# Self attention of layer 0: a head as four equal steps of scores, maxima, values and pieces

## The chip, the cores and the metric

The kernel runs on one core of a Trainium2 chip. The metric is device time in microseconds (us), the median of some runs. TensorE (PE) does the matmuls, VectorE (DVE), ScalarE (ACT) and GpSimd (POOL) the elementwise work, and SyncE (SP) issues nearly all transfers of this stage. Each engine works off its own instructions in their order; only weight loads (PEld) run beside matmuls.

## The reference, cut to what matters

Two decoder layers, each with self attention, cross attention and a feed-forward part, each followed by a sum with its input and a layer norm. The change touches the first self attention alone. Its input is x, 4 sequences of 1024 tokens with 256 features, and the reshape makes it 64 independent attentions of 1024 by 1024 with 64 features:

```python
SCALE = HEAD_DIM ** (-0.5)
bsz, seqlen, _ = x.shape
xq = jnp.einsum('bsh,oh->bso', x, wq)
xk = jnp.einsum('bsh,oh->bso', x, wk)
xv = jnp.einsum('bsh,oh->bso', x, wv)
xq = xq.reshape(bsz, N_HEADS, seqlen, HEAD_DIM)
...
scores = jnp.einsum('bhid,bhjd->bhij', xq, xk) * SCALE
scores = jax.nn.softmax(scores, axis=-1)
out = jnp.einsum('bhij,bhjd->bhid', scores, xv)
out = out.reshape(bsz, seqlen, N_HEADS * HEAD_DIM)
return jnp.einsum('bso,ho->bsh', out, wo)
...
x = _layernorm(x + _L0_attn_ref(x, L0_attn_wq, L0_attn_wk, L0_attn_wv, L0_attn_wo), axis=-1)
```

## The kernel before

`layer0_self_attention` (L301) takes 64 heads, in 16 groups of four (j = 0 to 3; GT = 256 tokens of x make one group). q and k are kept as a high and a low part in fp32r, and the products of scores are made of these. For a head the tiles are kA (high over low part of k), qA (high part of q twice), kB and qB (high part of k and low part of q; the first eight rows of kB are ones, those of qB the masked row maxima). Each is double buffered by the parity of the head.

A head does, per tile kc of 128 keys (kc = 0 to 7):
- scores (L614): two matmuls with kA, qA ("A") and two with kB, qB ("B"), all L627, into the four banks of psS, two for even and two for odd kc;
- the exponent (L639, ACT) from psS into pr, a ring of four tiles of 128x1024, and the sum of the exponents on POOL (add_up, L655; none for kc 0);
- values (L658): the product of pr and vd into psO (L667), 64 columns of the array for each half of the queries. These matmuls are fp32 and show as eight records for two kc.

Between them runs the work for the next head. largest (L567) takes 16 products (L579) of that head into the two banks of psX, of which VectorE takes the row maximum at once (L584); each waits for the maximum before the last. At the end of the head max_rows (L588) turns these maxima with two transposes into psX (L594), VectorE joins them (L599, L600), and masked (L605, L609) writes them into qB, half by half. The B matmuls of kc 0 wait for that.

The third kind of work are the pieces (misc, L395), products for a later group: 16 of Q and K in a group (L417: six matmuls, the high part taken out by ACT in L458, the low part by VectorE in L462, then sent to DRAM), V four times (L425, ACT L471), T, the transposes of x (L407), and O, the output product of two heads (L436, out by VectorE in L482, then moments, root and norm_out). S (L430) adds up the sums of exponents with ones; L475 turns it. They go to bank psM or, where it is free, to psX. Where they stand is the table SLOTS, by head and a name for the place; the waits for their bank are counted (`back`, `under`).

The order of a head before: scores 0 to 3 with largest 0 to 7, piece "1", values 0 and 1, S of the head before; scores 4 and 5 with largest 8 to 11, values 2 and 3, pieces "2" and "2b"; scores 6 and 7 with largest 12 to 15 (V pieces between); values 4 to 7; take_out (L677, psO to oU); max_rows; then the rest of the pieces, with the halves of masked among them:

```python
if more and not rest_first:
    masked(w, nb, 0)
    masked(w, nb, 1)
past_3 = piece("3")
if more and rest_first and (j, "3e") not in SLOTS:
    masked(w, nb, 0)
past_3b = piece("3b", bank=psX[:, 1, :], under=past_3)
if more and rest_first and (j, "3e") in SLOTS:
    masked(w, nb, 0)
```

rest_first holds where piece "3" is one of Q or K. Head 0 ends in two pieces and O, head 1 in four and V, head 2 in T and O, head 3 in five pieces. build (L531) fetches the tiles of the head after next when the last scores of a head are through: six transfers of 256 KB on SP, four of which (semaphore a0 or a1) the first L579 of the next head waits for. build_v (L556) fetches vd. divide (L696, POOL) applies the reciprocal of the sums.

## Time and profile before

| | before |
|---|---|
| median of 3 runs | 2968.56 us (2965.77 to 2969.53) |
| the profiled execution, its span | 2978.0 us |
| PE busy | 2631.8 us, 88% |
| DVE busy | 1704.5 us, 57% |
| POOL busy | 1621.4 us, 54% |
| ACT busy | 1190.8 us, 40% |
| adds of exponents, L655, 384 and 64 | 914.8 and 153.3 us |
| row maxima, L584, 1024 | 694.2 us |
| products of values, L667, 2048 records | 481.8 us |
| products of maxima, L579, 1024 | 415.8 us |

The busy times are of the whole program, of which the stage in question is the first 1760 us or so. The span is that of one profiled execution, the slices of the page cut it into 40 equal parts. A start time in a timeline is in us from the start of the span; where several equal instructions follow each other they are one row with a count.

### The profile page before, as it was taken

To read this page: it belongs to the slowest core of one execution; us is meant where nothing else is said; L and a number is where in the kernel's file an instruction comes from. 1 tells how busy PE (TensorE), PEld (TensorE's weight loads), DVE (VectorE), ACT (ScalarE), POOL (GpSimd) and SP (SyncE) were. 2 spreads that over 40 slices of the span, in tenths; PEclk is the share of its full clock that TensorE was granted. 3 is DMA by queue.
4 is the path that set the end of the run, shared out by engine and by line. 5 is a ranking of instruction groups with operands and counts; after the bars stand their busy time and mean duration, and the time that the engine had idled before them with its cause. 6 is when DMAs were issued, how large, how long until landed. Compare 5 with 4: busy or idle time off the path is not lost. (4 is left out here: it accounts for less than half of the span.)

```text
span 2978.0 us, 43667 instructions
## 1 busy us (share of the span) xinstructions
PE 2631.8 (88%) x12081; PEld 1634.0 (55%) x12081; DVE 1704.5 (57%) x3436; ACT 1190.8 (40%) x1678; POOL 1621.4 (54%) x1343
## 2 busy tenths in 40 slices
PE   7999999999999999999999968982795588798695
PEld 5666666666666666666666534441574244454254
DVE  5666666656666666665666635662234555468743
ACT  3444444444444444444444324541222333454234
POOL 3666776767766677676776753424334313333343
PEclk8999999999999999999999979996897599899798
DMA  6565455555446445455544320003993100000232
GB/s 176 113 136 113 105 120 113 123 115 114 109 113 138 108 109 121 109 122 114 118 112 108 76 68 23 2 2 126 343 347 128 41 0 1 30 2 9 61 116 88
DMA packets 407010, 303.20 MB, mean 102 GB/s; under 512 B 293558, under 2 KB 338910, under 8 KB 401790
## 3 DMA queue, kind: packets, MB, share of 16 engines
q1 hardware_dynamic: 390734, 231.17, 33.1%
q0 software_dynamic: 12224, 64.71, 6.1%
q10 hardware_dynamic: 3952, 6.08, 0.6%
q8 instruction: 51, 0.84, 0.1%
q14 instruction: 49, 0.40, 0.0%
HBM read 187.04 MB, written 94.39 MB: 95 GB/s over the span
## 5 line engine op out<-in xcount | busy, mean ns | idle before, releaser
L655 POOL TENSOR_TENSOR a_total<-a_total,a_pr 128x1024 f32<-128x1024 f32 x384 | 914.8, 2382 | 46.1 <-ACT a_pr L639 23.4
L639 ACT ACTIVATE a_pr<-a_psS 128x1024 f32<-128x1024 f32 x512 | 525.3, 1027 | 657.3 <-PE a_psS L627 657.3
L584 DVE TENSOR_REDUCE a_nmax<-a_psX 128x1 f32<-128x512 f32 x1024 | 694.2, 687 | 139.9 <-PE a_psX L579 137.8
L667 PE MATMUL a_psO<-a_pr,a_vd 128*64 128x512 f32 x2048 | 481.8, 602 | 0.0
L579 PE MATMUL a_psX<-a_kA,a_qA 128*128 128x512 f32 x1024 | 415.8, 408 | 17.3 <-issue 6.2
L655 POOL TENSOR_TENSOR a_total<-a_pr 128x1024 f32<-128x1024 f32 x64 | 153.3, 2396 | 487.9 <-ACT a_pr L639 487.9
L627 PE MATMUL a_psS<-a_qA,a_kA 128*128 128x512 f32 x1024 | 339.1, 412 | 2.5 <-DVE a_nT L600 1.4
L627 PE MATMUL a_psS<-a_qB,a_kB 128*128 128x512 f32 x1024 | 322.1, 396 | 0.0
L667 PEld LDWEIGHTS a_psO<-a_pr,a_vd 128*64 128x64 f32 x2048 | 129.9, 136 | 239.6 <-issue 188.1
L579 PEld LDWEIGHTS a_psX<-a_kA,a_qA 128*128 128x128 f32 x1024 | 193.9, 189 | 102.2 <-DVE a_nmax L584 23.5
L627 PEld LDWEIGHTS a_psS<-a_qA,a_kA 128*128 128x128 f32 x1024 | 181.2, 189 | 121.5 <-issue 90.1
L627 PEld LDWEIGHTS a_psS<-a_qB,a_kB 128*128 128x128 f32 x1024 | 193.6, 189 | 41.3 <-DVE a_qB L609 2.8
L599 DVE COPY a_nT<-a_psX 8x128 f32<-8x128 f32 x64 | 17.8, 278 | 222.4 <-PE a_psX L594 222.4
L1119 DVE TENSOR_REDUCE c_nmx<-c_psM 128x4 f32<-128x308 f32 x256 | 109.7, 469 | 50.9 <-PE c_psM L1114 50.0
L475 DVE STREAM_TRANSPOSE a_turned<-a_psM 128x512 f32<-128x512 f32 x64 | 45.9, 717 | 139.0 <-PE a_psM L430 139.0
L677 ACT ACTIVATE a_oU<-a_psO 128x512 f32<-128x512 f32 x64 | 38.4, 599 | 184.1 <-PE a_psO L667 180.1
L1103 POOL CAST c_qR<-c_qF 128x512 fp32r<-128x512 f32 x64 | 40.3, 632 | 113.7 <-ACT c_qF L1098 113.6
L609 DVE TENSOR_TENSOR a_qB<-a_nT,a_rowmask 8x512 fp32r<-8x512 f32 x128 | 99.3, 787 | 0.7
L1114 PE MATMUL c_psM<-c_kblk,c_qR 128*128 128x308 f32 x256 | 78.0, 369 | 23.5 <-DVE c_nmx L1119 10.1
L2607 ACT ACTIVATE e_hT<-e_psH,e_wt 128x128 f32<-128x128 f32 x160 | 45.7, 368 | 131.9 <-PE e_psH L2599 125.9
L1269 POOL TENSOR_TENSOR c_rstd<-c_mv,c_eps 128x2 f32<-128x2 f32 x32 | 6.6, 206 | 166.3 <-DVE c_mv L1259 166.3
L1114 PEld LDWEIGHTS c_psM<-c_kblk,c_qR 128*128 128x128 f32 x256 | 45.0, 193 | 90.2 <-issue 83.2
(400 smaller groups left out, 4517.5 us busy)
## 6 DMA issues: line engine op xcount, KB each, us to landing
a_qA<-a_qhi SPq DMA_DIRECT2D x124, 256.0 KB
a_vd<-a_vg SPq DMA_DIRECT2D x128, 128.0 KB
a_kA<-a_khi SPq DMA_DIRECT2D x62, 256.0 KB
a_kA<-a_klo SPq DMA_DIRECT2D x62, 256.0 KB
a_kB<-a_khi SPq DMA_DIRECT2D x62, 256.0 KB, 5.6
a_qB<-a_qlo SPq DMA_DIRECT2D x62, 256.0 KB, 5.9
a_qhi<-a_ph SPq DMA_DIRECT2D x120, 128.0 KB, 3.2
a_qlo<-a_pl SPq DMA_DIRECT2D x120, 128.0 KB, 2.7
```

The lines of the kernel that those rows point to most:

```text
L475: w.eng.transpose(turned[:, :], ps[:, :]).then_inc(sems["md"], 1)
L579: w.eng.matmul(psX[:, half, :], qA[:, b, u * P:(u + 1) * P], kA[:, b, half * 512:(half + 1) * 512], start=True, stop=True).then_inc(sems[" ...
L584: w.eng.tensor_reduce(nmax[:, half, u:u + 1], psX[:, half, :], AX.X, ALU.max, negate=True)\
L609: w.eng.tensor_tensor(qB[0:KC, b, cols].rearrange("p (u q) -> p u q", q=P), nT[:, 1, :].unsqueeze(1).to_broadcast([KC, KC // 2, P]), rowma ...
L627: last = w.eng.matmul(psS[:, half, q, :], kt[:, b, kc * P:(kc + 1) * P], qt[:, b, q * 512:(q + 1) * 512], start=a == 0, stop=a == 1)
L639: w.eng.activation(pr[:, n, :], psS[:, half, :, :].rearrange("p a b -> p (a b)"), ACT.Exp, scale=SCALE)\
L655: w.eng.tensor_tensor(total[:, buf, :], first, pr[:, n, :], ALU.add).then_inc(sems["ad"], 1)
L667: last = w.eng.matmul(psO[q * HD:(q + 1) * HD, :], vd[:, b, kc, :], pr[:, n, q * 512:(q + 1) * 512], start=kc == 0, stop=kc == KC - 1)
L1103: w.eng.tensor_copy(qR[:, n % 2, c, :], qF[:, n % 3, c, :]).then_inc(sems["qr"], 1)
L1114: w.eng.matmul(psM[:, k, 0:K4], qR[:, n % 2, c, tt * P:(tt + 1) * P], kblk[:, c, b, :, :].rearrange("p i k -> p (i k)"), start=True, stop= ...
L1119: w.eng.tensor_reduce(nmx[:, tt, 4 * c:4 * c + 4], psM[:, k, 0:K4].rearrange("p (i k) -> p i k", k=TK), AX.X, ALU.max, negate=True).then_i ...
L2607: last = w.eng.activation(hT[:, par, a, :], psH[:, par, a, :], GELU, bias=wt[:, slot, B1 + a:B1 + a + 1])
```

## The change

The table SLOTS and its places give way to TASKS, by head and step. A head is four equal steps p: scores 2p and 2p+1, with four of the 16 products of largest; then two kc of values, those of the step before (in step 0 kc 6 and 7 of the head before, and then take_out); S in step 1; then the pieces of the step. scores and exponent are apart. The pieces of Q and K: in head 3 two, none, two, four; in head 0 two, none, none, four; in head 1 two in step 0. V stands in step 2 of heads 0 and 1 and twice in that of head 2, O at the end of heads 1 and 2 (behind T there). With the last step go max_rows and masked: half 0 directly, half 1 directly or behind the third piece. moments stand in step 0, root in step 1, turn_back, divide and norm_out in step 2.

The waits for a bank are kept in `w.came`, the semaphore and count that took out what was last in it; room waits for that. build becomes two: build_keys behind step 1 (three transfers of half a tile, 128 KB) and build behind step 3 (nine of them; semaphore a needs its first four and the three of build_keys, b the other five). Before the loop eight pieces of Q and K are made for group 1, and sent by POOL, instead of five, and the waits of TensorE for all pieces ahead of the first head go. Shapes and number of the matmuls stay as they are.

```diff
-        AHEAD = 5
+        AHEAD = 8
         QK = [("Q", c) for c in range(KC)] + [("K", c) for c in range(KC)]
-        PLACES = [(3, "3"), (3, "3b"), (3, "3c"), (3, "3d"), (3, "3e"), (0, "1"), (0, "2"), (0, "2b"), (0, "3"), (0, "3b"),
-                  (1, "1"), (1, "3"), (1, "3b"), (1, "3c"), (1, "3e"), (2, "1")]
-        SLOTS = task_list()
+        PLACES = [(3, 0), (3, 0), (3, 2), (3, 2), (3, 3), (3, 3), (3, 3), (3, 3), (0, 0), (0, 0), (0, 3), (0, 3), (0, 3), (0, 3),
+                  (1, 0), (1, 0)]
+        TASKS = {place: [] for place in PLACES}
+        for place, task in zip(PLACES, QK, strict=True):
+            TASKS[place].append(task)
+        TASKS[0, 2], TASKS[1, 2], TASKS[2, 2] = [("V", 0, 0)], [("V", 0, 1)], [("V", 1, 0), ("V", 1, 1)]
+        TASKS[1, 3], TASKS[2, 3] = [("O", 1)], [("T",), ("O", 0)]
+        BANKS = {("QK", 2): "1M", ("QK", 4): "M10M", ("V", 1): "M", ("V", 2): "1M", ("O", 1): "M", ("T", 2): "1M"}
+        bank = {"0": psX[:, 0, :], "1": psX[:, 1, :], "M": psM[:, :]}
+        bank.update((f"S{i}", psS[:, i // 2, i % 2, :]) for i in range(4))
...
-        def misc(w, what, G, buf, more=True, bank=None, back=(0, 0), out=True):
+        def room(w, *places):
+
+            least = {}
+            for name, value in (w.came[k] for k in places if k in w.came):
+                least[name] = max(least.get(name, 0), value)
+            for name, value in least.items():
+                w.wait(name, w.at(name, w.count[name] - value))
+
+        def misc(w, what, G, buf, k="M", more=True, out=True):
 
 
             kind = what[0]
-            ps = psM if bank is None else bank
-            if w.on("tensor"):
-                w.wait("md", w.at("md", back[0]))
-                w.wait("ma", w.at("ma", back[1]))
+            ps = bank[k]
+            if w.on("tensor"):
+                room(w, k)
...
+            w.came[k] = ("ma", w.count["ma"]) if kind in "TV" else ("md", w.count["md"])
...
-        def build(w, G, j, b):
+        def halves(t, rows, b, h):
+            return t[rows:rows + HD, b, h * 512:(h + 1) * 512].bitcast(F32)
+
+        def build_keys(w, G, j, b):
+
 
             if w.on("sync"):
                 row = w.fixed(G * (GH * P) + j * P)
-                w.waits(("s", w.at("s")), ("sg", AHEAD * 2 * 16), ("sh", (PIECES - AHEAD) * 2 * 16), *((f"so{n}", w.at(f"so{n}")) for n in range(PIECES)))
-                for t, rows, src, n in ((qA, 0, qhi, "a"), (kA, 0, khi, "a"), (qA, HD, qhi, "a"), (kA, HD, klo, "a"),
-                                        (kB, HD, khi, "b"), (qB, HD, qlo, "b")):
-                    w.eng.dma_start(t[rows:rows + HD, b, :].bitcast(F32).rearrange("p (s n) -> p s n", n=512),
-                                    src[bass.ds(row, P), :].rearrange("(s p) n -> p s n", p=HD)).then_inc(sems[f"{n}{b}"], 16)
+                if j == 0:
+                    w.waits(("sg", AHEAD * 2 * 16), ("sh", (PIECES - AHEAD) * 2 * 16), *((f"so{n}", w.at(f"so{n}")) for n in range(PIECES)))
+                w.waits(("s", w.at("s")))
+                for t, rows, src in ((kB, HD, khi), (kA, 0, khi), (kA, HD, klo)):
+                    w.eng.dma_start(halves(t, rows, b, 0), src[bass.ds(row, HD), :]).then_inc(sems[f"a{b}"], 16)
+            w.inc(f"a{b}", 3 * 16)
+
+        def build(w, G, j, b):
+
+
+            if w.on("sync"):
+                row = w.fixed(G * (GH * P) + j * P)
+                w.waits(("s", w.at("s")))
+                for h, t, rows, src, n in ((0, qA, 0, qhi, "a"), (0, qA, HD, qhi, "a"), (1, kA, 0, khi, "a"), (1, kA, HD, klo, "a"),
+                                           (1, qA, 0, qhi, "b"), (1, qA, HD, qhi, "b"), (1, kB, HD, khi, "b"), (0, qB, HD, qlo, "b"),
+                                           (1, qB, HD, qlo, "b")):
+                    w.eng.dma_start(halves(t, rows, b, h), src[bass.ds(row + h * HD, HD), :]).then_inc(sems[f"{n}{b}"], 16)
             w.inc(f"a{b}", 4 * 16)
-            w.inc(f"b{b}", 2 * 16)
+            w.inc(f"b{b}", 5 * 16)
...
-        def largest(w, i, b, back=None):
+        def largest(w, i, b, first=False):
 
 
             u, half = i // 2, i % 2
             if w.on("tensor"):
                 if i == 0:
-                    w.wait(f"fa{b}", 8 * 16)
+                    if first:
+                        w.wait(f"fa{b}", 8 * 16)
+                        w.wait(f"fb{b}", 4 * 16)
                     w.wait(f"a{b}", w.at(f"a{b}"))
-                    w.wait("mn", w.at("mn"))
-                if back is not None:
-                    w.wait("md", w.at("md", back))
-                w.wait("mxr", w.at("mxr", 1))
+                elif i == KC:
+                    w.wait(f"b{b}", w.at(f"b{b}"))
+                room(w, "01"[half])
                 w.eng.matmul(psX[:, half, :], qA[:, b, u * P:(u + 1) * P], kA[:, b, half * 512:(half + 1) * 512],
                              start=True, stop=True).then_inc(sems["mx"], 1)
             w.inc("mx")
@@ -584,12 +612,13 @@
                 w.eng.tensor_reduce(nmax[:, half, u:u + 1], psX[:, half, :], AX.X, ALU.max, negate=True)\
                     .then_inc(sems["mxr"], 1)
             w.inc("mxr")
-
...
-        def scores(w, kc, b, a):
-
-            half = kc % 2
-            if w.on("tensor"):
-                if a == 0:
-                    if kc == 0:
-                        w.wait(f"fb{b}", 4 * 16)
-                        w.wait(f"b{b}", w.at(f"b{b}"))
-                    w.wait("e", w.at("e", 1))
-                kt, qt = (kB, qB) if a else (kA, qA)
-                for q in range(2):
-                    if a and kc == 0:
-                        w.wait("mb", w.at("mb", 1 - q))
-                    last = w.eng.matmul(psS[:, half, q, :], kt[:, b, kc * P:(kc + 1) * P], qt[:, b, q * 512:(q + 1) * 512],
-                                        start=a == 0, stop=a == 1)
-                if a:
-                    last.then_inc(sems["s"], 1)
-            if a == 0:
-                return
-            w.inc("s")
+        def scores(w, p, b, nb, first=False):
+
+
+            for kc in (2 * p, 2 * p + 1):
+                if w.on("tensor"):
+                    room(w, f"S{2 * (kc % 2)}", f"S{2 * (kc % 2) + 1}")
+                    w.wait("e", w.at("e", 1 - kc % 2))
+                for a, (kt, qt) in enumerate(((kA, qA), (kB, qB))):
+                    if w.on("tensor"):
+                        for q in range(2):
+                            if a and kc == 0:
+                                w.wait("mb", w.at("mb", 1 - q))
+                            last = w.eng.matmul(psS[:, kc % 2, q, :], kt[:, b, kc * P:(kc + 1) * P], qt[:, b, q * 512:(q + 1) * 512],
+                                                start=a == 0, stop=a == 1)
+                        if a:
+                            last.then_inc(sems["s"], 1)
+                    if nb is not None:
+                        largest(w, 2 * kc + a, nb, first)
+            for i in range(4):
+                w.came.pop(f"S{i}", None)
+            w.inc("s", 2)
+
+        def exponent(w, kc):
+
             n = w.count.get("e", 0) % RING
             if w.on("scalar"):
-                w.wait("s", w.at("s"))
-                w.wait("pv", w.at("pv", {0: 3, 1: 2}.get(kc, 1 - kc % 2)))
+                w.wait("s", w.at("s", 1 - kc % 2))
+                w.wait("pv", w.at("pv", 1 - kc % 2))
                 w.wait("ad", w.at("ad", 3 if kc in (0, 5, 6, 7) else 2))
-                w.eng.activation(pr[:, n, :], psS[:, half, :, :].rearrange("p a b -> p (a b)"), ACT.Exp, scale=SCALE)\
+                w.eng.activation(pr[:, n, :], psS[:, kc % 2, :, :].rearrange("p a b -> p (a b)"), ACT.Exp, scale=SCALE)\
                     .then_inc(sems["e"], 1)
             w.inc("e")
 
...
+            def tasks(j, p):
...
+                normal = j == 3 or (j == 2 and not first)
+                nG, nbuf = (G, 0) if j == 3 else (G - 1, 1)
+                for p in range(KC // 2):
+                    scores(w, p, b, nb if more else None, first and j == 0)
+                    for kc in (2 * p, 2 * p + 1):
+                        exponent(w, kc)
+                        add_up(w, kc, j % 2)
+                    if p == 0 and normal:
+                        moments(w, nbuf)
+                    if p == 0 and j == 2 and left >= 2:
+                        load_x(w, G + 2)
+                    if p == 1 and normal:
+                        root(w, nbuf)
+                    if p == 2 and old:
+                        turn_back(w)
+                        divide(w, (j - 1) % GH)
+                    if p == 2 and normal:
+                        norm_out(w, nG, nbuf)
+                    if not (last and j >= 2):
+                        if p == 1:
+                            build_keys(w, G + (j + 2) // GH, (j + 2) % GH, b)
+                        if p == 3:
+                            build(w, G + (j + 2) // GH, (j + 2) % GH, b)
+                    if p == 0:
+                        if old:
+                            values(w, KC - 2, nb)
+                            values(w, KC - 1, nb)
+                            take_out(w)
+                        if more:
+                            build_v(w, (j + 1) % GH, nb)
                     else:
...
                         values(w, 2 * p - 2, b)
                         values(w, 2 * p - 1, b)
-                        if p == 1 and old:
-                            misc(w, ("S",), G, (j + 1) % 2)
-                        if p == 1 and more:
-                            build_v(w, (j + 1) % GH, nb)
-                    if p == 2:
-                        under = piece("2")
-                        if w.on("tensor") and (j, "2b") in SLOTS:
-                            w.wait("mxr", w.at("mxr"))
-                        piece("2b", bank=psX[:, 1, :], under=under)
-                for kc in range(KC - 4, KC):
-                    values(w, kc, b)
-                take_out(w)
-                if more:
-                    max_rows(w, nb)
-                rest_first = left > 0 and SLOTS.get((j, "3"), ("T",))[0] in "QK"
-                if more and not rest_first:
-                    masked(w, nb, 0)
-                    masked(w, nb, 1)
-                past_3 = piece("3")
-                if more and rest_first and (j, "3e") not in SLOTS:
-                    masked(w, nb, 0)
-                past_3b = piece("3b", bank=psX[:, 1, :], under=past_3)
...
+                    if p == 1 and old:
+                        misc(w, ("S",), G, (j + 1) % 2)
+                    todo = tasks(j, p)
+                    if p == 3 and more:
+                        max_rows(w)
+                        masked(w, nb, 0)
+                        if not todo or todo[0][0][0] not in "QK":
+                            masked(w, nb, 1)
+                    for n, (task, g, buf) in enumerate(todo):
+                        kind = "QK" if task[0] in "QK" else todo[0][0][0]
+                        misc(w, task, g, buf, BANKS[kind, len(todo)][n] if len(todo) < 3 or kind == "QK" else "M")
+                        if p == 3 and more and n == 2:
+                            masked(w, nb, 1)
...
-            if w.role == "tensor":
-                w.wait("md", w.at("md"))
             for i in range(2 * KC):
-                largest(w, i, 0)
+                largest(w, i, 0, True)
...
             for i in range(AHEAD):
-                misc(w, QK[i], 1, 1, bank=psS[:, i // 2, i % 2, :] if i < 4 else psM[:, :], back=(i, 0))
+                misc(w, QK[i], 1, 0, ("S0", "S1", "S2", "S3", "M")[i % 5])
                 if i == 1:
-                    max_rows(w, 0)
+                    max_rows(w)
                     masked(w, 0, 0)
                     masked(w, 0, 1)
-            if w.role == "tensor":
-                w.wait("md", w.at("md"))
             group(w, 0, first=True)
...
+            values(w, KC - 2, 1)
+            values(w, KC - 1, 1)
+            take_out(w)
```

## Rows read from the trace of the kernel before

**Rows 1.** The page: the span, and the granted TensorE clock in 40 slices.

```profile
span 2978.0 us, 43667 instructions
PEclk8999999999999999999999979996897599899798
```

**Rows 2.** Four heads by stretches, 846.40 to 952.55: the sum; busy us of each engine.

```profile
sum 106.15, PE 105.51 PEld 67.32 DVE 65.43 ACT 45.53 POOL 73.63; mean PE 26.38 PEld 16.83 DVE 16.36 ACT 11.38 POOL 18.41
```

**Rows 3.** Timeline of PE: start, us, engine, line, operation, out<-in, shape, count; scores after O.

```profile
829.49 0.40 PE L579 MATMUL a_psX<-a_kA,a_qA 128*128 128x512 f32 x1
829.72 0.62 PE L627 MATMUL a_psS<-a_qA,a_kA 128*128 128x512 f32 x2
830.44 0.50 PE L579 MATMUL a_psX<-a_kA,a_qA 128*128 128x512 f32 x1
830.77 0.63 PE L627 MATMUL a_psS<-a_qB,a_kB 128*128 128x512 f32 x2
831.24 0.40 PE L579 MATMUL a_psX<-a_kA,a_qA 128*128 128x512 f32 x1
```

**Rows 4.** Timeline of PE, start of a head behind five pieces.

```profile
902.65 0.49 PE L579 MATMUL a_psX<-a_kA,a_qA 128*128 128x512 f32 x1
...
904.21 0.62 PE L627 MATMUL a_psS<-a_qA,a_kA 128*128 128x512 f32 x2
```

**Rows 5.** Timeline of PE, pieces and the product O behind them.

```profile
821.16 0.40 PE L417 MATMUL a_psX<-a_xl,a_wkh 128*128 128x256 f32 x2
821.40 0.40 PE L417 MATMUL a_psX<-a_xh,a_wkl 128*128 128x256 f32 x2
822.02 3.72 PE L436 MATMUL a_psM<-a_wo,a_oT 128*128 128x256 f32 x16 [0.22 <-DVE a_pl L462]
```

**Rows 6.** Timeline of PE, a short block of values and the long one.

```profile
837.64 0.39 PE L579 MATMUL a_psX<-a_kA,a_qA 128*128 128x512 f32 x1
...
839.83 0.74 PE L627 MATMUL a_psS<-a_qA,a_kA 128*128 128x512 f32 x2
840.41 0.40 PE L579 MATMUL a_psX<-a_kA,a_qA 128*128 128x512 f32 x1
...
842.49 0.39 PE L579 MATMUL a_psX<-a_kA,a_qA 128*128 128x512 f32 x1
...
846.40 0.38 PE L594 MATMUL a_psX<-a_ident,a_nmax 128*8 128x128 f32 x2
```

**Rows 7.** Line L609, 100 to 1600: duration in ns, min/median/max, first and last start.

```profile
L609 DVE TENSOR_TENSOR a_qB<-a_nT,a_rowmask x114: 669/670/1450, 105.3 to 1593.2; 8x512 fp32r<-8x512 f32 x114
```

**Rows 8.** Timeline of POOL and of DVE, end of a head 3.

```profile
896.76 4.84 POOL L655 TENSOR_TENSOR a_total<-a_total,a_pr 128x1024 f32<-128x1024 f32 x2
...
900.98 1.17 DVE L609 TENSOR_TENSOR a_qB<-a_nT,a_rowmask 8x512 fp32r<-8x512 f32 x1
```

**Rows 9.** Timeline, all engines: the B pair of a kc and its exponent.

```profile
1701.39 0.63 PE L627 MATMUL a_psS<-a_qB,a_kB 128*128 128x512 f32 x2
...
1702.05 1.02 ACT L639 ACTIVATE a_pr<-a_psS 128x1024 f32<-128x1024 f32 x1 [0.37 <-PE a_psS L627]
```

**Rows 10.** Timeline, PE and DVE: the transposes of the maxima and the masks.

```profile
1691.63 0.38 PE L594 MATMUL a_psX<-a_ident,a_nmax 128*8 128x128 f32 x2
...
1692.67 3.43 DVE L609 TENSOR_TENSOR a_qB<-a_nT,a_rowmask 8x512 fp32r<-8x512 f32 x2
```

**Rows 11.** Timeline of PE, last group: last B pair and the next head's first L579.

```profile
1687.26 0.62 PE L627 MATMUL a_psS<-a_qB,a_kB 128*128 128x512 f32 x2
...
1695.26 0.67 PE L579 MATMUL a_psX<-a_kA,a_qA 128*128 128x512 f32 x1 [1.84 <-issue]
```

**Rows 12.** Transfers issued from 800 to 1000: count, KB each, median us to landing.

```profile
a_kB<-a_khi SPq DMA_DIRECT2D x7, 256.0 KB, 5.6
...
y_scratch<-a_res SPq DMA_DIRECT2D x4, 128.0 KB, 1.7
```

**Rows 13.** Timeline of PE, start of the second head.

```profile
82.63 0.47 PE L579 MATMUL a_psX<-a_kA,a_qA 128*128 128x512 f32 x1 [1.45 <-issue]
```

102 lines of the change are left out of this document (29 added, 73 removed).

## The prediction

> **What bounds the kernel now.** I read the page first. Its slices show that the first stage, the self attention of layer 0, fills the first 24 of 40, at a granted TensorE clock of 0.9 or more of full speed, and that nothing behind it uses a line of the diff; the chain of the page speaks of the last stage only, so it is no help here [rows 1]. The table by stretches, cut at the transposes of L594 (one per head), is the view to trust: the four heads of a group take 106.15 us, TensorE is busy for 105.51 of them, VectorE for 65, ScalarE for 46 and GpSimd for 74 [rows 2]. So a head costs what TensorE's program costs, and another engine counts only where TensorE waits for it. Busy time hides short waits, because the ends of matmuls are modelled; I read the distance from one start to the next instead. In a run of scores that is 0.23 for one L579 (829.49 to 829.72) and 0.47 for a pair of L627 (830.77 to 831.24) [rows 3].
>
> **What the change removes.** The number and shape of all products stay: no line changes values(), S, the transposes or the pieces (values still fill 64 columns at a time), so any gain must come from waits. I find three kinds.
> (a) Where a head is entered after the product O, eight L579 in a row run into VectorE, which has the result of O and its moments between the maxima: the pair at 829.72 takes 0.72 for 0.47 and the L579 behind it 0.33 for 0.23, so 0.36 in all. Two heads of a group, 16 groups: 11.5 us. After the change only four L579 stand in a row, and the moments stand behind them, beside a block of values. I count this as gone.
> (b) Behind the five pieces at the end of head 3 the next head goes from 902.65 to 904.21, 1.56 for 0.23+0.47+0.23, so 0.63 lost [rows 4]; 14 groups, 8.8 us.
> (c) O waits for a piece in its own bank: 0.62 for 0.24, so 0.38 [rows 5]; 15 groups, 5.7 us. It gets a head end without pieces, and what was in its bank before was taken out long ago.
> Together 26 us.
>
> **What it adds: a fourth block of half array products.** Before, a head has values 0-1 (with S), 2-3 and 4-7; after, 6-7, 0-1 with S, 2-3 and 4-5. Crossing between the whole array and the halves is paid in each. A short block (8 products) goes from 837.64 to 839.83, less 0.23 for the L579 itself: 1.96; the pair of scores behind it then takes 0.58, 0.12 too much. The long one (16) goes from 842.49 to 846.40, less 0.23: 3.68, and the transposes behind it pay nothing [rows 6]. Two short ones are 1.96+0.12+1.96=4.04, so the split costs 0.36, in 63 heads 22.7 us. No reason is in the trace for less: each of the three blocks of a head pays it now.
> The Trainium skill has two rules that speak here against each other. "TensorE: Matmul & The Clock Gate" (Step-by-step) says that the engine loads weights ahead of running matmuls; by that alone the fourth block is free and the sum 22.7 us lower. "TensorEngine Tiling (Array Packing)" (Key Properties) says that a change of tiling mode drains the engine. The distances above side with the second.
>
> **What it moves: the mask before the pieces.** This is the largest term. At the end of a head the row maxima are turned, then L609 writes them into qB in two halves. Before, the halves stand behind the first pieces on VectorE; after, masked(0) stands ahead of all of them. L609 reads two operands from SBUF, as does GpSimd's add L655. The median of 114 masks is 0.67, the longest 1.45 [rows 7]. Where one meets an add, it ends 0.55 behind that add: POOL's pair of adds ends at 901.60, the mask that began at 900.98 at 902.15 [rows 8]. Now the clock of the new end of head 3 or head 0, from the start of scores 6:
> scores 6 are A 0.46, L579 0.23, B pair from 0.69; the exponent starts 0.66 behind the start of that pair and takes 1.02 [rows 9]: it ends at 2.4. Adds take 2.4 each [rows 8]: the add of 6 runs from 2.5 to 4.9, that of 7 from 4.9 to 7.3. TensorE ends scores 7 at 2.8, does its short block until 4.7 and turns the maxima. The mask starts 1.04 behind the transposes (1691.63 to 1692.67) [rows 10], at 5.8, in the middle of the last add: it ends at 7.85. Before, four kc of values stood there, and the mask meets the adds in one head of each group, that of rows 8.
> Who waits for that: VectorE is in order, so piece 0 is taken out (0.42) only by 8.3. TensorE needs that for the fourth piece, which has bank M again; it ends three pieces, nine pairs 0.24 apart [rows 5], at 4.7+0.2+3x0.72=7.1. So it stands for 1.2. The reductions of the next head start late and cost 0.1 more. In head 3 the root of the norm (four small POOL operations, 1.3 us) and the division push the adds by another 0.3 to 0.4. I take 1.5. It happens behind head 3 (14 times) and head 0 (15): 43 us. Its bounds: nothing, if the add is out of the way; 2.4 (a whole further add) if POOL is later than I think, 70 us. I take the middle because both ends of the overlap have room: the mask would have to start 0.9 earlier or 1.5 later to miss that add. Behind heads 1 and 2 stands O (3.3 us), under which both masks fit; no cost.
> The Trainium skill ("SBUF — State Buffer", Who interferes with whom) has it that a VectorE instruction with two SBUF inputs and a GpSimd instruction that reads SBUF exclude each other for a whole instruction. The trace agrees.
>
> **What else moves.** The tiles of the head after next are now fetched by 12 transfers of half the size in place of 6, three of them after step 1 and nine after step 3. SyncE has room, since none of its steps is asked for sooner than a step later, except the four that the first L579 of the next head needs. From the pair of scores 7 to that L579 now pass up to 8.0 us (1687.26 to 1695.26), where a head end without other work shows the transfers alone in the way [rows 11]. After the change, behind O of head 1, the window from the end of scores 7 is 6.1, as two kc of values less stand in it; behind head 2 6.6, behind pieces 6.8 and more. Transfers of 256 KB land 5.6 after issue with others before them in the queue, one of 128 KB after 1.7 [rows 12]. Half the bytes, and four issues in place of four twice as long: I take 5 and call it hidden; the other end is no gain in speed, 1.1 at most behind head 1, 0.6 behind head 2 and less elsewhere, 14x1.1+16x0.6+32x0.2 to 0.4, some 30 us in all.
> Setting up: eight pieces in place of five before the first head is the same work earlier. One wait of 1.45 at the second head may go, since half the bytes are in its transfers [rows 13]; with the wait for all pieces ahead of the first head, I count 2 us less. The last two groups have head ends without pieces, where masks and adds meet anyway: TensorE leaves one block of values less there and pays it later, 1 us in two places, 2 us more. POOL bounds the very last head in both.
>
> **Sum.** -26 (waits) +22.7 (fourth block) +43 (mask) -2 +2 = +39.7 us. The profiled execution has 2978.0; the median of the runs is 2968.56, 9.4 lower, and I add the difference to the median: 3008.3. A group in the middle should take 106.15-(2x0.36+0.63+0.38)+4x0.36+2x1.5=108.9.
>
> **Rivals.**
> 1. The mask doesn't meet the add, or the piece doesn't wait for the mask: 43 us fall away and the sum is -5: 2964, not slower. It decides itself at the start of masked(0): before 4.9 or after 7.3 in the clock above. For it: three of four head ends now are clean. Against it: these have 1.7 us more of values ahead. 0.17.
> 2. The fetch of the next head's tiles is late (it takes the place of the waits that went): up to +30, 3038. For it: the present slack is 1 us or less in a plain head end. Against it: half the bytes. 0.12.
> 3. The blocks cost nothing more, by the weights loaded ahead: 3008.3-22.7=2985.6. Against it: rows 6. 0.04.
> 4. The pace of single matmuls changes, as it varies from 0.226 to 0.236 within a head for no cause that I can name: 0.004 on some 216 of them in a group is 14 us: 2994, or 2951 together with rival 1. 0.05, 0.03 of it on the fast side.
> The forecast: 0.60, with its own range from 2994 to 3023 (a stall of 1.0 to 2.0 in 29 places). 0.02 is left for what makes it faster and stands nowhere above.
>
> **How the numbers follow.** A difference under 0.2%, 5.9 us, can't be told from none here. Faster: rival 1 has -5 with some 4 either way, so 0.08 of its 0.17, with 0.03 of rival 4 and the 0.02: 0.13. Same: the other 0.09 of rival 1. Slower: the rest, 0.78. The range must reach to rival 1 and most of the way to rival 2: 2962 to 3030.
>
> **What would show it.** Between transposes: heads 3 and 0 longer, heads 1 and 2 about as now, group 108.9. In the lines: L609 at 1.5 to 2.1 in half of its first halves, a wait of L417 for L462 of some 1.2, 29 times; no wait of L579 for a reduction inside a step. A wait of L579 for the tiles of kA would be rival 2. I am wrong if the masks stay at 0.67, or if the group is under 106.

## The result, and the profile after

| | before | after |
|---|---|---|
| median | 2968.77 us (2965.77 to 2969.53, 4 runs) | 3036.55 us (3033.16 to 3042.03, 4 runs) |
| profiled span | 2978.0 us | 3035.6 us |
| VectorE busy | 1704.5 us | 1802.9 us |
| masks of the row maxima, 128 (L609, now L639) | 99.3 us, 787 ns each | 185.9 us, 1472 ns each |

The ratio is 1.0229, 95% interval 1.0213 to 1.0246: slower by 67.8 us, where 39.7 had been forecast, and above the upper end of the range, 3030. The sign was right and the size was not.

The four heads that answer to [rows 2], from the transposes at the end of one head 1 to those at the end of the next (the table by stretches; the columns are the busy time and the count of each engine, the granted clock, the share of the DMA engines, GB/s):

```profile
core 0: us, PE busy (x) PEld busy (x) DVE busy (x) ACT busy (x) POOL busy (x), PEclk, DMA share, GB/s
882.36:910.50 28.14, 26.58 (x116) 16.30 (x114) 16.88 (x27) 10.48 (x12) 18.86 (x13) 1.00 0.29 89
910.50:937.62 27.12, 27.12 (x132) 17.31 (x131) 18.94 (x32) 11.91 (x16) 18.71 (x13) 1.00 0.42 110
937.62:965.26 27.64, 26.34 (x131) 16.40 (x129) 18.21 (x29) 11.69 (x16) 18.08 (x9) 1.00 0.50 125
965.26:992.66 27.40, 26.28 (x130) 16.45 (x128) 17.98 (x29) 11.70 (x16) 17.87 (x9) 1.00 0.50 124
sum 110.30, PE 106.32 PEld 66.46 DVE 72.00 ACT 45.78 POOL 73.52; mean PE 26.58 PEld 16.61 DVE 18.00 ACT 11.45 POOL 18.38
```

The group takes 110.30 us for 106.15, and 108.9 had been forecast. TensorE is busy for 0.8 more and stands still for 3.98 in place of 0.64. VectorE's busy time has grown by 6.57. Three of the four stretches have a hole in TensorE's row of 1.1 to 1.6 us, and only the second has none.

The waits of TensorE (waiting operation and its line, what released it, us in total, times, longest) name the holes:

```profile
PE a_psM L426 <- DVE a_pl L472: 35.1, 29, 1.4
PE a_psO L701 <- DMA a_vd<-a_vg: 20.9, 15, 1.6
...
PE a_psX L607 <- issue: 5.9, 1, 5.9
```

The first is the piece (L426) that waits until VectorE has emptied its bank, 29 times as forecast. The second stood nowhere in the forecast: the first product of values of a head waits for a transfer into vd. The third is the first product of the program's first head.

The first hole, at the end of a head 3 (timelines of DVE, POOL and PE; start, us, engine, line):

```profile
828.31 2.44 DVE L639 TENSOR_TENSOR a_qB<-a_nT,a_rowmask 8x512 fp32r<-8x512 f32 x1
830.68 0.41 DVE L472 TENSOR_TENSOR a_pl<-a_psM,a_ph 128x256 fp32r<-128x256 f32 x1
...
825.37 4.84 POOL L689 TENSOR_TENSOR a_total<-a_total,a_pr 128x1024 f32<-128x1024 f32 x2
...
829.39 0.40 PE L426 MATMUL a_psX<-a_xh,a_wql 128*128 128x256 f32 x2
831.14 0.50 PE L426 MATMUL a_psM<-a_xh,a_wqh 128*128 128x256 f32 x2 [1.35 <-DVE a_pl L472]
```

It answers to [rows 8] and reads as the forecast has it: the mask begins at 828.31, GpSimd's pair of adds ends at 830.21, the mask at 830.75, 0.54 behind it; only then is piece 0 taken out, and the fourth piece, due at 829.63, starts at 831.14. That is 1.51 lost; behind head 0 it is 1.28; the pair behind each hole takes 0.35 for 0.24 (831.14 to 831.49), another 0.1. Over 100 to 1600 the median of the masks is 1378 ns where [rows 7] has 670. Behind heads 1 and 2 the first half of the mask is as long (median 2.17 and 2.18), but no piece of Q or K waits behind it there.

The second hole, in step 1 of a head 2 (timelines of SyncE's queue and of PE):

```profile
890.64 0.40 SPq L391 DMA_DIRECT2D a_xg<-x  x1
891.14 0.42 SPq L393 DMA_DIRECT2D a_xs<-x  x1
891.74 1.14 SPq L589 DMA_DIRECT2D a_vd<-a_vg  x2
...
893.43 0.40 PE L607 MATMUL a_psX<-a_kA,a_qA 128*128 128x512 f32 x1
895.38 1.94 PE L701 MATMUL a_psO<-a_pr,a_vd 128*64 128x512 f32 x8 [1.56 <-DMA a_vd<-a_vg]
```

The transfers that are awaited here are not those that values 0 read. build_v in step 0 fetches the values of the next head, into the buffer that values 7 of the old head leave. The values that values 0 multiply were fetched a head earlier, and landed by 867.3. The two pairs of transfers (instructions of one line: count, min/median/max in ns, first and last start):

```profile
L589 SPq DMA_DIRECT2D a_vd<-a_vg x2: 506/548/591, 864.4 to 864.9; - x2
...
DMA to landing us min/median/max: 2.2/2.3/2.4
```

```profile
L589 SPq DMA_DIRECT2D a_vd<-a_vg x2: 495/542/590, 891.7 to 892.3; - x2
...
DMA to landing us min/median/max: 3.1/3.1/3.1
```

The second pair lands at 895.34, and values 0 start at 895.38. The reason is in the wait of values(), which the change left as it was:

```python
if kc == 0:
    w.wait("bv", w.at("bv"))
```

w.at counts all transfers that the program has issued so far. In the kernel before, build_v stands behind values 0 and 1 in step 1, so the count takes in only the head's own; now it stands in step 0, and the count takes in the next head's too. Those are late in head 2 for two reasons: they can't be issued before values 7 are through (888.90+1.94=890.84), and the fetch of x stands ahead of them on SyncE until 891.56. No piece stands in this step 0 to cover the wait. So values 0 start 1.95 behind the L607 ahead of them, where 0.32 is usual: 1.63 in each group.

The third, the first product of maxima of all, after and before (timeline of PE):

```profile
40.42 1.19 PE L607 MATMUL a_psX<-a_kA,a_qA 128*128 128x512 f32 x2 [5.92 <-issue]
```

```profile
36.18 0.92 PE L579 MATMUL a_psX<-a_kA,a_qA 128*128 128x512 f32 x2 [2.26 <-DMA a_kA<-a_pl]
```

The change makes it wait for all twelve transfers of the first head and not for the eight that it reads, and the first transposes come 4.5 us later, at 56.75 for 52.27.

### The profile page after: what moved, and what is told of

It reads as the page before. It is cut to its first block and busy times, and to the rows that moved or that the text cites. A ratio compares the mean times of both kernels' runs of the same rounds, so it can differ in the third digit from the quotient of the medians.

```text
span 3035.6 us, 43749 instructions
## 1 busy us (share of the span) xinstructions
PE 2638.9 (87%) x12081; PEld 1616.4 (53%) x12081; DVE 1802.9 (59%) x3436; ACT 1194.3 (39%) x1678; POOL 1622.4 (53%) x1349
## 5 line engine op out<-in xcount | busy, mean ns | idle before, releaser
L701 PE MATMUL a_psO<-a_pr,a_vd 128*64 128x512 f32 x2048 | 496.7, 606 | 21.0 <-DMA a_vd<-a_vg 20.9
L607 PE MATMUL a_psX<-a_kA,a_qA 128*128 128x512 f32 x1024 | 410.3, 402 | 13.6 <-issue 5.9
L656 PE MATMUL a_psS<-a_qA,a_kA 128*128 128x512 f32 x1024 | 336.1, 409 | 0.2 <-DVE a_pl L472 0.2
L656 PE MATMUL a_psS<-a_qB,a_kB 128*128 128x512 f32 x1024 | 322.9, 396 | 4.1 <-DVE a_qB L639 4.0
L607 PEld LDWEIGHTS a_psX<-a_kA,a_qA 128*128 128x128 f32 x1024 | 194.6, 190 | 80.2 <-DVE a_nmax L612 11.4
L656 PEld LDWEIGHTS a_psS<-a_qA,a_kA 128*128 128x128 f32 x1024 | 180.5, 189 | 99.3 <-issue 70.6
L656 PEld LDWEIGHTS a_psS<-a_qB,a_kB 128*128 128x128 f32 x1024 | 193.5, 189 | 43.8 <-DVE a_qB L639 6.4
L639 DVE TENSOR_TENSOR a_qB<-a_nT,a_rowmask 8x512 fp32r<-8x512 f32 x128 | 185.9, 1472 | 2.2
L472 DVE TENSOR_TENSOR a_pl<-a_psX,a_ph 128x256 fp32r<-128x256 f32 x120 | 47.3, 413 | 124.8 <-ACT a_ph L468 124.8
L446 PE MATMUL a_psM<-a_wo,a_oT 128*128 128x256 f32 x512 | 117.6, 383 | 3.3 <-POOL a_oT L730 3.3
L446 PEld LDWEIGHTS a_psM<-a_wo,a_oT 128*128 128x128 f32 x512 | 96.0, 193 | 17.4 <-issue 5.0
L468 ACT ACTIVATE a_ph<-a_psM 128x256 fp32r<-128x256 f32 x119 | 45.7, 384 | 130.9 <-PE a_psM L426 130.9
```

Source lines behind the costliest of these rows:

```text
L446: last = w.eng.matmul(ps[:, 0:D], oT[:, buf, c, :], wo[:, c, :], start=c == 0, stop=c == KC - 1)
L607: w.eng.matmul(psX[:, half, :], qA[:, b, u * P:(u + 1) * P], kA[:, b, half * 512:(half + 1) * 512], start=True, stop=True).then_inc(sems[" ...
L639: w.eng.tensor_tensor(qB[0:KC, b, cols].rearrange("p (u q) -> p u q", q=P), nT[:, 1, :].unsqueeze(1).to_broadcast([KC, KC // 2, P]), rowma ...
L656: last = w.eng.matmul(psS[:, kc % 2, q, :], kt[:, b, kc * P:(kc + 1) * P], qt[:, b, q * 512:(q + 1) * 512], start=a == 0, stop=a == 1)
L701: last = w.eng.matmul(psO[q * HD:(q + 1) * HD, :], vd[:, b, kc, :], pr[:, n, q * 512:(q + 1) * 512], start=kc == 0, stop=kc == KC - 1)
```

## The experiments

All medians are set against runs of the kernel before on the same chip. What stands over it is the ratio less one, times 2969 us.

| run | median us | ratio, 95% interval | over the kernel before |
|---|---|---|---|
| the changed kernel | 3036.55 | 1.0229 (1.0213 to 1.0246) | +68 |
| e2_mask_psum | 3009.88 | 1.0134 (1.0114 to 1.0155) | +40 |
| e3_mask_late | 3004.73 | 1.0117 (1.0096 to 1.0137) | +35 |
| e7_before_mask_first | 3010.84 | 1.0129 (1.0113 to 1.0144) | +38 |
| e4_vd_four | 3012.97 | 1.0144 (1.0118 to 1.0170) | +43 |
| e5_first | 3035.95 | 1.0206 (1.0185 to 1.0226) | +61 |
| e10_three_mended | 2989.50 | 1.0046 (1.0031 to 1.0061) | +14 |
| e6_four_blocks | 3042.71 | 1.0222 (1.0201 to 1.0243) | +66 |
| e1_values_home | 3001.44 | 1.0109 (1.0089 to 1.0130) | +32 |
| e9_home_apart | 3120.05 | 1.0495 (1.0476 to 1.0513) | +147 |
| e11_apart_early | 2978.86 | 1.0017 (1.0007 to 1.0027) | +5 |
| e12_pair_early | 2954.83 | 0.9961 (0.9948 to 0.9974) | -12 |

**The mask: where it reads, and what is queued behind it.** The same wait was attacked from two sides. First the operand:

```diff
-w.eng.tensor_tensor(nT[:, 1, :], nT[:, 0, :], psX[0:KC, 0, P:2 * P], ALU.min)
+w.eng.tensor_tensor(psX[0:KC, 0, 2 * P:3 * P], nT[:, 0, :], psX[0:KC, 0, P:2 * P], ALU.min)
...
-                    nT[:, 1, :].unsqueeze(1).to_broadcast([KC, KC // 2, P]),
+                    psX[0:KC, 0, 2 * P:3 * P].unsqueeze(1).to_broadcast([KC, KC // 2, P]),
...
                         masked(w, nb, 0)
-                        if not todo or todo[0][0][0] not in "QK":
-                            masked(w, nb, 1)
+                        masked(w, nb, 1)
...
+            w.came["0"] = ("mb", w.count["mb"])
```

> The changed kernel, except that the minimum of the two halves of the row maxima is written to PSUM, so that the mask (L639) reads one operand from PSUM and one from SBUF, as the reductions do; both masks of a head stand behind one another, and the bank they read is free only after both. Everything else, the blocks and the add on GpSimd, is as in the changed kernel. Theory (the mask waits for the whole GpSimd add because both read two operands in SBUF): the masks go back to about 0.7 in all heads, the fourth piece's stall of 1.3 to 1.5 us mostly goes; a part of it comes back since the second mask (0.7) now stands ahead of the pieces: -14 to -28 us, 3008 to 3022. Rival (the mask is long for another reason: the wait on its inputs, its own write to qB, or the place in the order): first halves stay above 2 us, and with the second ahead of the pieces the time is 3036 or more, up to 3056.

The masks of e2 (costliest groups: busy us, mean ns) and the wait that is left:

```profile
L639 DVE TENSOR_TENSOR a_qB<-a_psX,a_rowmask 8x512 fp32r<-8x512 f32 x128 | 81.7, 673 | 2.2
...
PE a_psX L426 <- DVE a_qB L639: 16.5, 29, 0.6
```

The 128 masks take 673 ns on average, among the same adds and with the same work in them: 126 of them begin while an add of the exponents runs, and in the changed kernel the 67 that do take 2.2 us on average. So the long masks of the changed kernel are not their place or their size: a VectorE instruction with two operands in SBUF stands for as long as GpSimd's add runs, and one with a single SBUF operand doesn't. This is what the Trainium skill has in "SBUF — State Buffer" (Who interferes with whom). The time fell by 28 us, the upper end of what was expected, though a wait of 0.6 in 29 places came in for the second mask, as expected. Then the order:

```diff
-                        masked(w, nb, 0)
-                        if not todo or todo[0][0][0] not in "QK":
+                        if not todo or todo[0][0][0] not in "QK":
+                            masked(w, nb, 0)
                             masked(w, nb, 1)
...
-                        if p == 3 and more and n == 2:
-                            masked(w, nb, 1)
+                        if p == 3 and more and kind == "QK" and n in (1, 2):
+                            masked(w, nb, n - 1)
```

> The changed kernel, with one order changed on VectorE: behind heads 3 and 0, where four pieces stand, the first half of the mask stands behind the second piece's remainder and the second half behind the third's, in place of ahead of all pieces. What it costs is the same where it meets the last add, but no piece is queued behind it at the time. Theory (29 stalls of the fourth piece of 1.3 to 1.6 us come from the mask that is queued ahead of the first piece): the stall goes nearly whole, -28 to -40 us, 2997 to 3009; the mask itself may still be up to 1.5 us where it meets the rest of the add. Rival (the piece waits for its bank for another cause, such as ScalarE's copy): the stall and the time stay, 3030 to 3040. Rival 2 (the mask now comes too late for the first products of the next head that use it): a wait of L656 for the mask of some 0.5 us in 29 places, 3010 to 3020.

33 us less, inside 28 to 40. The same head end as above, in e3:

```profile
817.13 0.42 DVE L472 TENSOR_TENSOR a_pl<-a_psM,a_ph 128x256 fp32r<-128x256 f32 x1 [0.54 <-ACT a_ph L468]
...
818.20 0.86 DVE L639 TENSOR_TENSOR a_qB<-a_nT,a_rowmask 8x512 fp32r<-8x512 f32 x1
...
817.72 0.40 PE L426 MATMUL a_psX<-a_xh,a_wql 128*128 128x256 f32 x2
817.96 0.40 PE L426 MATMUL a_psM<-a_xh,a_wqh 128*128 128x256 f32 x2
```

Piece 0 is taken out first, the fourth piece follows the third by 0.24, and the mask (0.86 here, 1.12 on average) holds up no piece. The start of the next head pays a part: from its first pair of scores to its second L607 it takes 1.70 for 1.16. A group gets 2.2 shorter, of the 3.0 that the holes take, so three quarters of the stall are the queue behind the mask, and the rest comes back at the start of the head. And the other way round, the same order in the kernel before:

```diff
-                if more and not rest_first:
+                if more:
                     masked(w, nb, 0)
```

> The kernel before with one order changed on VectorE: at the end of head 3, and of each other head where pieces stood ahead of the mask, the first half of the mask stands ahead of all pieces. Its blocks, pieces and transfers stay, so that four kc of values still stand between scores 7 and the mask. Theory (the order costs only where the mask meets an add, and the mask meets one only because the changed kernel brings it 1.7 us forward): the masks stay at 0.67 in three heads of a group, and at 1.2 at most in head 3 with a stall of up to 0.6 there, 14 times: 0 to +9, 2968 to 2980. Rival (the order costs by itself: any mask ahead of the pieces holds up the fourth one): +20 or more, 2990.

Its 38 us are the rival's number, and the theory's 0 to 9 us are refuted. At the end of a head 3 (timelines of DVE and PE), where the adds end at 812.47:

```profile
810.22 2.79 DVE L609 TENSOR_TENSOR a_qB<-a_nT,a_rowmask 8x512 fp32r<-8x512 f32 x1
...
813.40 0.51 PE L417 MATMUL a_psM<-a_xh,a_wqh 128*128 128x256 f32 x2 [1.69 <-DVE a_pl L462]
```

I had held that the mask meets the add because 1.7 us of values were taken away ahead of it. With those values in place it still meets it in two head ends of a group, behind heads 3 and 1 (first masks of 2.79 and 2.10, and 0.67 in the other two): the pieces that stood ahead of it on VectorE had kept it out of the add. There the next stretch grows by 1.3. Behind head 0, where only two pieces stand, the mask is ahead of them too, keeps its 0.67, and the stretch grows by 0.1. So what the runs bear out of the theory is that the order costs where the mask meets the add. The values alone bring it into the add as well: behind head 2 both kernels have the mask ahead of T and O, and its first half (median) goes from 0.68 to 2.18. Either edit can bring it into the add; its place ahead of pieces of Q and K makes that cost.

**The transfer of the values.**

```diff
-        vd = m.sb("vd", [P, 2, KC, HD])
+        vd = m.sb("vd", [P, GH, KC, HD])
...
+                    if p == 0 and more:
+                        build_v(w, (j + 1) % GH, (j + 1) % GH)
```

> The changed kernel, with four buffers of vd in place of two, so that the transfers of the values of the next head need not wait for values 7 of the old head, and with their issue at the start of step 0, ahead of the fetch of x. Nothing else is moved. Theory (values 0 of head 2 wait 1.6 us in each of 14 groups, because the transfer is issued too late): that wait is gone and nothing takes its place: -22 to -25, 3012 to 3015. Rival (the wait hides one that follows, such as values 0 waiting for the sum of the head before to be taken out, or x and the tiles come later as they now stand behind vd in the queue): -10 or less, 3027 or more.

25 us less. The edit does two things, since with four buffers the transfers can also be issued ahead of the fetch of x; values 0 still wait for the next head's transfers, which now land in time. So it shows what the wait costs, and not which of its causes would have to go. That a wait for the head's own transfers alone would do, in one line and with two buffers, follows from the landings above and was not tried. The wait list of e4 has 0.9 us for vd where the changed kernel has 20.9, and the wait for the pieces unchanged:

```profile
PE a_psM L426 <- DVE a_pl L472: 35.3, 29, 1.3
...
PE a_psO L701 <- DMA a_vd<-a_vg: 0.9, 2, 0.8
```

**The first head.**

```diff
-                        w.wait(f"fb{b}", 4 * 16)
...
                             if a and kc == 0:
+                                if q == 0:
+                                    w.wait(f"fb{b}", 4 * 16)
```

> The changed kernel, except that the first head's products of maxima wait for the B half of its tiles (four transfers) only where B is first read, and not ahead of their first A product. Theory (the first transposes come 4.5 us later than before because of this wait): -3.6 to -4.5 us, 3032 to 3033, the first transposes at 52 to 53. Rival (the eight pieces ahead of the first head, or their transfers, are late anyway): no change, first transposes at 56 or later.

The transposes came at 52.69, as expected, but the time shows nothing that can be told from none: 0.6 us by the medians, 7 by the ratios, whose intervals overlap. In the trace the gain is given back within the same head:

```profile
65.47 0.40 PE L606 MATMUL a_psX<-a_kA,a_qA 128*128 128x512 f32 x1
69.64 3.43 PE L703 MATMUL a_psO<-a_pr,a_vd 128*64 128x512 f32 x8 [3.78 <-DMA a_vd<-a_vg]
```

Values 0 wait until 69.64, where the changed kernel has them at 70.86, and take 3.43 for 1.94, at a granted clock of 0.56; the transposes at the end of that head come at 84.06 for 83.77. In the changed kernel it is again the next head's transfer that they wait for (it lands at 70.81, their own at 50.07). What was late was not only what the change waited for. In the middle of the stage (transposes at 880.82 for 882.36) 1.5 us are left of it.

**Do the parts add up?** The three edits together, e3, e4 and e5.

> The changed kernel with three edits together: the mask's halves behind the second and the third piece, four buffers of vd issued at the start of step 0, and the wait for the B half of the first head's tiles put back to its first use. Its four blocks of half-array products stay. Theory (the losses are separate and add up): 3036.6 -31.8 (mask) -23.6 (values' transfers) -4.5 (first head) = 2976.7, range 2970 to 2984, so about 0.2% over the kernel before, since the fourth block (22.7) and the waits removed (26) cancel. Rival (the stalls hide one another, so that a part of one gain is lost): over 2985.

The median is on the rival's side; set against the kernel before of its own call (2973.5) it is 54 us less than the changed kernel, between the 60 of the theory and the 52 that the rival allows. A group in the middle (805.44 to 912.01) takes 106.57, within 0.42 of the kernel before and within 0.2 of what e3 (2.2) and e4 (1.7) take off 110.3, so there the parts add up. The miss is in the first group, which is 8.9 longer than before, with the wait for vd of e5 still in it (2.57 at 68.60).

**The block of half-array products, in the kernel before.**

```diff
+                        if kc == 6:
+                            values(w, 4, b)
+                            values(w, 5, b)
...
-                for kc in range(KC - 4, KC):
-                    values(w, kc, b)
+                values(w, KC - 2, b)
+                values(w, KC - 1, b)
```

> The kernel before with one edit: values 4 and 5 of every head stand behind scores 6, ahead of scores 7, so that a head has four blocks of half-array products in place of three. No mask, piece or transfer is moved. Theory (each block costs 0.36 us of changing between the whole array and halves): 63 or 64 times 0.36 = +22.7 to +23, about 2992 (2988 to 2997). What may come on top or off: the scores 7 end 1.8 us later, and the last add with them. Rival (weights are loaded ahead, a further block is free): 2966 to 2972. Rival 2 (the later end of scores 7 moves the last add into the mask): over 3000, with masks L609 over 1.3 us in more than one head of a group.

66 us, far over the theory, and the masks stay at 712 ns, so rival 2 has the number alone. Two places of one group (timeline of PE):

```profile
926.29 1.94 PE L667 MATMUL a_psO<-a_pr,a_vd 128*64 128x512 f32 x8
928.16 0.72 PE L627 MATMUL a_psS<-a_qA,a_kA 128*128 128x512 f32 x2
...
929.74 2.11 PE L667 MATMUL a_psO<-a_pr,a_vd 128*64 128x512 f32 x8
931.78 0.38 PE L594 MATMUL a_psX<-a_ident,a_nmax 128*8 128x128 f32 x2
...
935.60 0.63 PE L627 MATMUL a_psS<-a_qA,a_kA 128*128 128x512 f32 x2
937.22 0.49 PE L579 MATMUL a_psX<-a_kA,a_qA 128*128 128x512 f32 x1 [0.99 <-DMA a_kA<-a_klo]
```

The new block takes 1.87; the last one takes 2.04, of which 0.17 is a wait for exponent 7, which now has too little in front of it. By whole heads, those that don't start behind pieces are longer by 0.5 to 0.6, and with the 0.17 taken off that is about the 0.36 that was forecast for a block. A group is longer by 3.9: 4x0.36 for the blocks, 4x0.17 for the exponent, and 1.8 in the two heads that start behind pieces. There the first L579 waits, as at 937.22. The other 11 us are in the first and the last group. The wait list of e6 against that of the kernel before:

```profile
PE a_psX L579 <- DMA a_kA<-a_klo: 18.7, 13, 2.5
...
PE a_psX L579 <- DVE a_pl L462: 8.3, 12, 0.9
```

```profile
PE a_psX L579 <- DVE a_pl L462: 2.8, 12, 0.2
...
PE a_psX L579 <- DMA a_kA<-a_klo: 0.5, 1, 0.5
```

That is 23.7 us more, of 14x1.8=25. The part put down to L462 is a wait for the tiles as well, as far as the traces tell: in the kernel before, the same L579 starts (851.34) ahead of the L462 in question (851.49). It is the mechanism of the prediction's second rival: one block less behind scores 7, and the tiles that are fetched from then on come late. In the changed kernel the same wait is 4.9 us in all, 3 times, with tiles of half the size; that their size is what saved it was not tried by itself.

**The values back home.** With the losses named, a kernel should beat both that keeps the waits removed and not the blocks. First only values 6 and 7 were moved back:

```diff
-                    if p == 0:
-                        if old:
-                            values(w, KC - 2, nb)
-                            values(w, KC - 1, nb)
-                            take_out(w)
-                        if more:
-                            build_v(w, (j + 1) % GH, nb)
-                    else:
+                    if p > 0:
                         values(w, 2 * p - 2, b)
                         values(w, 2 * p - 1, b)
+                    if p == 3:
+                        values(w, KC - 2, b)
+                        values(w, KC - 1, b)
+                        take_out(w)
```

> The changed kernel with one thing undone: values 6 and 7 of a head and the taking out of its sum stand again at the end of their own head (step 3, ahead of the turned maxima), in place of step 0 of the next. The order of the end is otherwise the new one: both halves of the row maxima ahead of the pieces, two pieces a step, the transfers in 128 KB. So TensorE has three blocks of half-array products in a head (the last of 16), the mask starts some 1.7 us later and behind the last add, and the values' transfers can be issued at the start of step 0. Theory (the loss of the change is the mask that meets GpSimd's last add, the fourth block, and the wait for the values' transfers): -22.7 (block) -40 (stalls of the fourth piece) -24 (wait for the values) from 3036.6: about 2950, range 2945 to 2965; the row maxima's masks at 0.67 us in all heads, no wait of the pieces for VectorE, no wait for vd. Rival 1 (the mask is long because of its new place ahead of the pieces, not because of the add): masks stay near 2.2, the stall stays, about 2990. Rival 2 (the quarter-size transfers or the pieces two a step cost by themselves): above 2975, with waits for kA's tiles or psM.

3001, 51 us over what I expected and outside its range. It is in the range of the second rival, but neither kA's tiles nor psM are waited for as it would have it. The masks are at 0.68 (median of 114), the wait of the fourth piece is gone, that for vd is 1.8 us in all, and a wait has come that I had not thought of (timeline of PE in step 0, and the wait list):

```profile
793.03 0.39 PE L607 MATMUL a_psX<-a_kA,a_qA 128*128 128x512 f32 x1
794.28 0.50 PE L426 MATMUL a_psX<-a_xh,a_wqh 128*128 128x256 f32 x2 [0.86 <-DVE a_nmax L612]
...
PE a_psX L426 <- DVE a_nmax L612: 36.4, 44, 0.9
```

In step 0 nothing stood any more between the products of maxima and the first piece, which takes over the bank of the last one: 1.25 for 0.23, three times in a group. So the fourth block was not mere loss, it covered the reductions. The next edit puts one piece behind scores 0 and one behind scores 1, both in bank M, and takes in e5's wait:

```diff
+                    apart = p == 0 and len(tasks(j, p)) == 2
...
+                        if apart:
+                            scores(w, p, b, nb if more else None, first and j == 0, (kc,))
                         exponent(w, kc, apart)
                         add_up(w, kc, j % 2)
+                        if apart:
+                            task, g, buf = tasks(j, p)[kc]
+                            misc(w, task, g, buf, "M")
```

> The kernel with values 6 and 7 at their own head's end (2 blocks' worth of its miss named there), the wait for the B half of the first head's tiles put back to its first use, and one more edit in step 0 of heads 3, 0 and 1: the two pieces stand one behind scores 0 and one behind scores 1, both in bank M, in place of both behind scores 1 in banks 1 and M. Theory (the 31 us by which the kernel without this edit is still over the one before are three waits a group, of 0.9 to 1.0 us each, of the first piece for the reduction of the maxima whose bank it takes over, which the values stood in front of in the changed kernel): these waits go, one more change between scores and pieces costs 0.1 in each place, so 45 times 0.9 = 40 us less than 3001.4, and 4 less for the first head: 2957, range 2948 to 2968, under the kernel before by 0.2 to 0.7%. Rival (VectorE or ScalarE is simply late in step 0 whatever the order, so that the wait comes back at the next product of maxima or at the third scores): 2985 to 2998.

Here the theory and its rival both missed, by 120 us and more. The waits for the reduction are gone, and scores and pieces of step 0 run without a gap. But build_v() is called behind them now, and on SyncE's queue:

```profile
907.45 0.48 SPq L502 DMA_DIRECT2D a_klo<-a_pl  x1
908.11 1.15 SPq L589 DMA_DIRECT2D a_vd<-a_vg  x2
...
908.21 0.39 PE L606 MATMUL a_psX<-a_kA,a_qA 128*128 128x512 f32 x1
911.25 3.53 PE L704 MATMUL a_psO<-a_pr,a_vd 128*64 128x512 f32 x8 [2.65 <-DMA a_vd<-a_vg]
```

the transfers of the next head's values stand behind the sends of the pieces, the last of which wait for VectorE, and values 0 wait for them. It is the error of the prediction once more, in a kernel of my own. One line was moved:

```diff
+                    if p == 0 and more:
+                        build_v(w, (j + 1) % GH, nb)
                     apart = p == 0 and len(tasks(j, p)) == 2
```

> e9_home_apart with one line moved: the transfers of the next head's values (vd) are issued at the very start of step 0, ahead of the two pieces of that step, whose sends wait on SyncE for VectorE's remainder. Theory (the 3120 us of e9 are the waits for vd alone, 2 to 3.4 us each in three heads of a group, and the slow clock behind them, since its issue had slipped behind the sends of the pieces): the waits go, the pieces of step 0 stay without theirs, a group in the middle takes 105.6 us (116.1 less 10.5), 0.5 less than in the kernel before, and the first group some 5 more: 2960, range 2952 to 2968. Rival (VectorE or ScalarE is late in step 0 once the waits for vd no longer give it time; the waits come back as waits of L606 or L658 for the reduction): 2975 to 2998.

2979: 141 us came back, and 5 are left over the kernel before. That is outside the range of 2952 to 2968 and in the rival's, but not by its waits. A group takes 106.2 and not 105.6, since values 0 still wait up to 0.5 for vd in two heads, and in the first head for 5.3. With four buffers of vd, the transfers of two heads at a time in step 2, ahead of the tiles of step 3, and those of the first head ahead of the tiles of the second in the prologue:

```diff
+                    if p == 2 and j % 2 and not (last and j == 3):
+                        build_v(w, (j + 1) % GH, (j + 1) % GH)
+                        build_v(w, (j + 2) % GH, (j + 2) % GH)
```

> e11_apart_early with the transfers of the values taken out of the full stretch of SyncE's queue: vd has four buffers, and those of two heads are issued together in step 2 of heads 1 and 3, ahead of the tile transfers of step 3; in the prologue those of head 0 stand ahead of the tiles of head 1. Nothing else is moved. Theory (what e11 still loses is the wait of values 0 for vd: 0.5 and 0.17 in two heads of a group and 5.3 in the first head, with the slow clock behind it): -0.67x15=-10 and -8 in the first group from 2978.9: 2961, range 2953 to 2967, 0.2 to 0.5% under the kernel before. Rival (the tile transfers, or the reductions in step 0, are late by the same time behind it, so the wait moves to L606): 2972 to 2980.

2954.8, ratio 0.9961 (0.9948 to 0.9974): faster than both kernels, at the lower end of what was expected. Four heads of it by stretches, against [rows 2] and the table above:

```profile
sum 105.58, PE 105.08 PEld 66.70 DVE 65.01 ACT 45.28 POOL 73.61; mean PE 26.27 PEld 16.68 DVE 16.25 ACT 11.32 POOL 18.40
```

VectorE is back at 65, and no wait for vd is left. A group is 0.6 shorter than before, some 8 us over the fourteen, and the last group, up to its last transposes, is 4 shorter (71.1 for 75.3); which of the edits does the latter was not tried.

## Why the prediction was wrong

Step by step, in its order.

**The waits removed, -26.** Right. In the changed kernel no L607, L656 or O waits in the places of [rows 3 to 5].

**The fourth block, +22.7.** Right as far as the runs tell: every head has four blocks, and e6 has about 0.36 a head once its wait for the exponent is taken off.

**The mask, +43.** Right in mechanism, place, count and size. 29 waits, 1.51 and 1.28 with 0.1 behind each, 14x1.61+15x1.38=43.2 us where 1.5 each had been taken. One sign was off: the first halves are 2.2 to 2.4 in all four head ends, and not 1.5 to 2.1 in half of them, which costs nothing behind heads 1 and 2. e2 shows the add as the cause, e3 the queue behind the mask as what makes it cost. One reason given for it was incomplete: the 1.7 us of values were not needed for it, as e7 shows.

**"SyncE has room, since none of its steps is asked for sooner than a step later".** This is the step that failed. It was worked out for the tiles of kA, qA, kB and qB alone, and vd has no term in the sum. Moving build_v from behind values 0 to step 0 puts the next head's transfers into the count that values 0 wait for, so that they are asked for one step after their issue and not a head later; and with values 7 in step 0 they can't be issued before its end. In head 2, with the fetch of x ahead and no piece to cover it, that is 1.63 in each group, 21 us in the list of waits, and 25 that e4 gives back. How the 1.63 divides was not tried. An estimate from the starts above: without the fetch of x the transfers could be issued up to 0.9 sooner (890.84 for 891.74), and with a wait for the head's own transfers, in place by 867.3, nothing would be left.

**Setting up, -2.** Wrong in sign: +4.5 at the first transposes, and another 6.5 in the first group where 2.75 was forecast for a group. The change has the first product wait for four more transfers, and I had counted only that half the bytes are in each. e5 shows that this wait sets the first transposes, and that the values' transfer takes most of the gain back; what else makes the first group long was not tried alone.

**The last groups, +2.** From the transposes of 1704.69, where the last group begins, to the end of the stage 1.8 us are lost; no run tests it by itself.

**The sum.** A group was forecast at +2.75 and is +4.15. Adding 1.63 for vd gives 4.38, so 0.23 stays unexplained. Over the stage, from the traces: 4.5 to the first transposes, 6.5 in the first group, 52.6 in the next fourteen (the last of them shorter), 1.8 behind, 65.5 in all, beside 67.8 by the medians.

**The rivals.** The mask did meet the add (rival 1 out). The tiles were in time (rival 2 out for the changed kernel, and at work in e6). Blocks did cost (rival 3 out). The pace of single matmuls stayed: from an L579, now L607, to the pair behind it the median is 0.231 in both kernels (rival 4 out). Rival 1's own figure doesn't add up: without the 43 us the sum is -3.3, and not -5, which would be 2965. The number 3038 of rival 2 is close to the result, by another transfer: the list of what a moved step feeds was one entry short. And the upper end of the range was cut at 3030, though that rival's price of 30 was there to be taken in whole.
